# One Trainium2 core, a two-layer perceiver block: the first cross attention's queries widened from one stacked operand

## What is computed

```python
q_hk   = (layernorm(x) @ Wq.T).reshape(B, S, 16, 128)
q_big  = einsum('bshk,hkq->bshq', q_hk, w_kc_q)     # 384 wide
q_r    = einsum('bshq,hqr->bhsr', q_big, W_qr)      # 64 wide
k_r    = einsum('bld,hdr->bhlr', kv_r, W_kr)        # 64 wide
scores = einsum('bhsr,bhlr->bhsl', q_r, k_r)
```

## Time and profile before

| | |
|---|---|
| median of three runs | 2110.57 us |
| the profiled execution | 2113.88 us |
| its span, first to last instruction | 2112.1 us |
| mean granted TensorE clock | 0.982 of full speed |
| PE busy over the span | 94% |
| first queries (turning of rows to the last widen) | about 10 to 120 us |

### The profile page before, as it was taken

One profiled execution on the slowest core, in us unless ns is written; L12 is line 12 of the kernel. 1 busy time (PEld: TensorE's weight loads), 2 busy tenths in 40 slices (PEclk: granted clock), 3 DMA queues, 4 the chain that ended last, 5 costly groups with the idle time before them and its releaser, 6 DMA issues. The chain is left out here.

```text
span 2112.1 us, 29249 instructions
## 1 busy us (share of the span) xinstructions
PE 1982.2 (94%) x9274; PEld 1436.9 (68%) x9274; DVE 1202.1 (57%) x2691; ACT 868.3 (41%) x2163; POOL 1005.4 (48%) x928
## 2 busy tenths in 40 slices
PE   7989999999999999999997999989978999999996
PEld 6858998876688744666664899877755555555553
DVE  4577787467651022666656878769863343444444
ACT  3555555233312100344334555535514444454451
POOL 1257884212352100566667788475303444555552
PEclk9999999999999999999999999999988999999999
DMA  5552331200311100122134233210345999888886
GB/s 186 194 191 63 97 100 61 82 1 1 120 52 43 35 0 0 42 91 78 58 105 146 64 97 101 87 68 1 104 152 153 312 299 327 211 214 217 216 212 183
DMA packets 104948, 251.47 MB, mean 119 GB/s; under 512 B 14800, under 2 KB 40912, under 8 KB 96304
## 3 DMA queue, kind: packets, MB, share of 16 engines
q1 hardware_dynamic: 82224, 196.02, 27.5%
q0 software_dynamic: 21136, 51.11, 11.4%
q10 hardware_dynamic: 1440, 2.49, 0.3%
HBM read 279.44 MB, written 55.07 MB: 158 GB/s over the span
## 5 line engine op out<-in xcount | busy, mean ns | idle before, releaser
L99 PE MATMUL banks<-L1f_w,L1f_xT 128*128 x760 | 265.0, 492 | 1.8 <-issue 1.3
L2967 POOL DMA_INDIRECT moe_sums<-L1f_y,L1f_row x94 | 149.4, 1589 | 218.5 <-DVE L1f_is_who L2834 169.8
L99 PEld LDWEIGHTS banks<-L1f_w,L1f_xT 128*128 128x128 f32 x760 | 138.0, 192 | 81.6 <-issue 6.7
L160 POOL TENSOR_TENSOR rstd<-rstd,power 128x1 f32<-128x1 f32 x48 | 32.0, 667 | 221.4 <-DVE rstd L154 221.4
L2785 DVE SCALAR_TENSOR_TENSOR L1f_z<-banks,L1f_share,L1f_sg 128x192 f32<-128x192 f32 x95 | 39.7, 418 | 147.9 <-ACT L1f_sg L2718 146.9
L2975 POOL DMA_INDIRECT L1f_xg<-moe_rows,L1f_row x95 | 94.4, 993 | 61.5 <-DVE L1f_spare L2825 24.6
L2718 ACT ACTIVATE L1f_sg<-banks 128x192 f32<-128x192 f32 x95 | 31.4, 331 | 206.1 <-PE banks L99 143.3
L99 PE MATMUL banks<-L0f_down,L0f_z 128*128 128x512 f32 x256 | 111.1, 592 | 1.5 <-DVE L0f_z L2242 1.5
L99 PE MATMUL banks<-L0f_hT_hi,L0f_ug_hi 128*128 128x512 f32 x256 | 100.0, 391 | 0.0
L99 PE MATMUL banks<-L0f_hT_hi,L0f_ug_lo 128*128 128x512 f32 x256 | 99.6, 389 | 0.0
L99 PE MATMUL banks<-L0f_hT_lo,L0f_ug_hi 128*128 128x512 f32 x256 | 99.6, 389 | 0.0
(11 more groups left out here) (433 smaller groups left out, 5701.5 us busy)
## 6 DMA issues: line engine op xcount, KB each, us to landing
L1f_w<-in_experts SPq DMA_DIRECT2D x95, 1280.0 KB
L1f_laid<-moe_counts SPq DMA_DIRECT2D x59, 512.0 KB
w<-in_L1x_heads SPq DMA_DIRECT2D x16, 704.0 KB, 4.0
L0x_q<-L0x_far SPq DMA_DIRECT2D x20, 512.0 KB
L1x_q<-L1x_far SPq DMA_DIRECT2D x20, 512.0 KB
w<-in_L0x_heads SPq DMA_DIRECT2D x8, 1216.0 KB, 6.5
L0x_far<-L0x_away_far SPq DMA_DIRECT2D x8, 1024.0 KB
w<-in_wug SPq DMA_DIRECT2D x8, 1024.0 KB, 4.8
```

The costliest lines, as they stand in the source:

```text
L99: ins = pe.e.matmul(out, w, m, start=first and n == 0, stop=last and n == len(pairs) - 1)
L160: pool.e.tensor_tensor(self.rstd[:, i:i + 1], self.rstd[:, i:i + 1], self.power[:, 0:1], ALU.pow).then_inc(self.rstd_set.sem, 1)
L2967: pool.e.indirect_dma_start(self.sums[j % 2][:, :], bass.IndirectOffsetOnAxis(ap=self.row[:, j:j + 1], axis=0), self.y[j % self.NY][:], No ...
```

## The change

`qr_hi` and `qr_lo` of 128 rows are replaced by one operand per head of the pair, `qr[t][e]`: rows 0 to 63 hold the leading half of that head's q_r, rows 64 to 127 its remainder. So `qr_high` is two copies of 64 rows by 512 columns, and `qr_low` two subtractions of 64 rows by 512 columns (the second copy moves rows 64 to 127 to rows 0 to 63, the first subtraction the other way). The host packs `kr` twice, in rows 0 to 63 and 64 to 127. `widen` then takes two matmuls a head: `kr_hi` on all 128 rows by the stacked operand (hi by hi and hi by lo at once), and `kr_lo` on 64 rows by the stacked operand's upper 64 rows. `kr_lo` is made for 64 rows. Signals are counted twice as fast, to the same points. Order, banks, loads and sizes of loads are as before.

```diff
-            self.qr = [tuple(sb(f"qr_{v}{i}", [P, BANK], F32R) for v in ("hi", "lo")) for i in range(2)]
+            self.qr = [[sb(f"qr{i}_{e}", [P, BANK], F32R) for e in range(2)] for i in range(2)]
...
     def widen(self, pe, g, t):
...
-        pe.wait_ge(self.qr_hi, n + 1)
-        pe.wait_ge(self.qr_lo, n + 1)
+        pe.wait_ge(self.qr_hi, 2 * n + 2)
+        pe.wait_ge(self.qr_lo, 2 * n + 2)
...
+        hi, lo = self.kr[g % 2]
         for e in range(2):
-            ins = accumulate(pe, self.q_bank(t, e), parts(cut(self.kr[g % 2], slice(None), slice(e * DC, (e + 1) * DC)),
-                                                          cut(self.qr[t], slice(None))))
+            at, both = slice(e * DC, (e + 1) * DC), self.qr[t][e]
+            ins = accumulate(pe, self.q_bank(t, e), [(hi[:, at], both[:]), (lo[0:RR, at], both[0:RR, :])])
...
     def qr_high(self, act, g, t):
...
-        act.e.copy(self.qr[t][0][:], self.ask_bank(t)).then_inc(self.qr_hi.sem, 1)
+        for e in range(2):
+            act.e.copy(self.qr[t][e][0:RR, :], self.ask_bank(t)[e * RR:(e + 1) * RR, :]).then_inc(self.qr_hi.sem, 1)
...
     def qr_low(self, dve, g, t):
-        hi, lo = self.qr[t]
-        dve.wait_ge(self.qr_hi, 2 * g + t + 1)
-        dve.e.tensor_tensor(lo[:], self.ask_bank(t), hi[:], ALU.subtract).then_inc(self.qr_lo.sem, 1)
+        n = 2 * g + t
+        dve.wait_ge(self.qr_hi, 2 * n + 2)
+        for e in range(2):
+            both = self.qr[t][e]
+            dve.e.tensor_tensor(both[RR:P, :], self.ask_bank(t)[e * RR:(e + 1) * RR, :], both[0:RR, :],
+                                ALU.subtract).then_inc(self.qr_lo.sem, 1)
...
-            pool.e.tensor_tensor(lo[:], self.w(g, "kr").rearrange("p e n -> p (e n)"), hi[:], ALU.subtract).then_inc(self.kr_lo.sem, 1)
+            pool.e.tensor_tensor(lo[0:RR, :], self.w(g, "kr").rearrange("p e n -> p (e n)")[0:RR, :], hi[0:RR, :],
+                                 ALU.subtract).then_inc(self.kr_lo.sem, 1)
...
-            kr_t[1::2, RR:], kr_t[1::2, 0:RR] = kr_t[1::2, 0:RR].copy(), 0.0
+            kr_t[:, RR:] = kr_t[:, 0:RR]
```

More of the change, by code:

```diff
@@ L725, in __init__ @@
         self.asked, self.widened = take("asked", 2 * n), take("wide_again", 2 * n)
-        self.qr_hi, self.qr_lo = take("qr_hi", 2 * n), take("qr_lo", 2 * n)
+        self.qr_hi, self.qr_lo = take("qr_hi", 4 * n), take("qr_lo", 4 * n)
         self.query_signals()
@@ L792, in fold_ready @@
         if h == 0:
-            pe.wait_ge(self.qr_hi, 2 * n - 1)
-            pe.wait_ge(self.qr_lo, 2 * n - 1)
+            pe.wait_ge(self.qr_hi, 4 * n - 2)
+            pe.wait_ge(self.qr_lo, 4 * n - 2)
         elif h == 1:
@@ L873, in ask @@
         pe.wait_ge(self.h_lo, (t + 1) * NT // 2)
-        pe.wait_ge(self.qr_hi, 2 * (g - 1) + t + 1)
-        pe.wait_ge(self.qr_lo, 2 * (g - 1) + t + 1)
+        pe.wait_ge(self.qr_hi, 2 * (2 * (g - 1) + t + 1))
+        pe.wait_ge(self.qr_lo, 2 * (2 * (g - 1) + t + 1))
         accumulate(pe, self.ask_bank(t), [p for k in range(KD) for p in parts(
```

## The result

The changed kernel has a median of 2119.22 us (2115.99 to 2122.27, six runs) beside 2109.78 us of the kernel before in the same comparison: ratio 1.0046, 95% interval 1.0031 to 1.0062. Run again with the other experiments it had 2121.40 beside 2111.19, ratio 1.0051 (1.0034 to 1.0069). It is slower, by 9 to 10 us, where 5.6 were forecast. 2119.22 lies in the range, just under its upper end of 2120; the 2121.40 of the second comparison would lie above it. The time came into the range by a narrow margin.

A forecast was written before the change was run, and what follows sets the result against it. TensorE was taken to bound the stage from about 42 to 117 us. Pair 0 +0.8, widens up to ask(6, 0) +3.65, the write chain +0.97 and widen(7, 1) +0.15 gave +5.6 us: 2116.2 us, range 2108.5 to 2120.

The forecast's parts named there:

- Tile changes: In widen on TensorE, each switch between 128 and 64 rows costs 0.20 us; four make +0.35 us a widen net.
- A: Switches in widen cost nothing beside long matmuls: -4.05 us, 2106.5; chance 0.12.
- A2: Switches in widen cost half, 0.10 us each, so a widen stays level: +0.8 us in all, 2111.4; chance 0.10.
- B: Each switch in widen costs its upper price, 0.35 us: +0.96 a widen, +12.8 us, 2123.4; chance 0.10.
- a widen of 1.71 us: Timeline sign: widen takes 1.71 us to the next step's start, with starts about 0.33, 0.43, 0.43 and 0.43 apart.
- The 0.216 us: Skill page's distance between 512-column matmuls, by columns alone; by it 32 matmuls removed would gain 6.9 us.
- The 7.3 us saved: On TensorE, 16 widens drop from six matmuls to four: 32 fewer at 0.227 us each.
- Pair 0: At the stage's start, the longer split on ACT and DVE starts ask(0, 1) 0.9 us later; counted as +0.8 us.
- 64 rows cost what 128 do: ACT copies and DVE subtractions on 64 rows take as long as on 128, some 0.48 and 0.60 us back to back.
- Pair 7: At the stage's end, the chain through SP's write adds +0.97 us up to widen(7, 1), then +0.15 in it.
- the clock: TensorE is at 1.2 GHz from 31 to 34 us; if it recovers when it did, ask(0, 1)'s delay counts +0.8 us.
- The same: Outcome class of a time within about 0.3% (6.3 us) of the kernel before; chance 0.60, against slower 0.36, faster 0.04.

The follow-up runs named there:

- the grouped order: Changed kernel with widen's four products ordered 128, 128, 64, 64 rows, so two tile changes instead of four: 2116.58 us beside 2110.91, 1.0024.
- that order at pair 0: Changed kernel, second product on 128 rows; in pair 0 ACT and DVE split the last two row tiles before q_r of ask(0, 0): 2106.96 us beside 2110.82.
- the order at pair 7: 128-row second product and pair 0 reordered; in pair 7, q_r of ask(7, 1) split before keeping widen(6, 1)'s queries: 2105.19 us beside 2111.19.
- pair 0's order: Kernel before, only pair 0 reordered: ACT and DVE split the last two row tiles before q_r of ask(0, 0): ratio 0.9993.

## Why the forecast named the mechanism and came out too small

*Tile changes, 0.20 us each, four a widen:* right, in the middle pairs to the hundredth (12.05 us a pair), and shown by three kernels with the stacked operand that have zero, two and four of them (10.44, 11.27, 12.05 us), and by one that has them and nothing else of the change (12.95). Rivals A, A2 and B are out: they put a pair at 10.4, 11.3 and 13.3 us. One sign was written down wrong: a widen of 1.71 us "from its first start to the next step's" does not fit the four starts beside it, which add up to 1.62. Measured are 1.60, and the last 0.11 lies behind the fold's first start. (Rival B's +0.96 a widen should be +0.95; nothing hangs on it.) The 0.216 us that the prediction took from the Trainium skill's page "TensorE: Matmul & The Clock Gate", section "Back-to-back issue gap", is given there for an isolated matmul; for a stream of weight loads and matmuls the same section gives about 0.131 at 512 columns, which no run here shows. The stream measured 0.227.

*The 7.3 us saved are real:* without tile changes a pair is 0.91 us shorter. But only what is saved ahead of SP's write reaches the end. Behind it TensorE waits 4 us for the chain of write, copies and subtractions at pair 7.

*Pair 0, sized 0.9 us later:* the step that was too small is "64 rows cost what 128 do", with two operations back to back at "some 0.48 and 0.60 us". One operation costs that, but two on halves of the rows don't overlap with their neighbours. DVE from rows_lo(6) to rows_lo(7) is 31.09 - 28.93 = 2.16 us, where it was 1.21 before:

```profile
28.52 0.69 DVE L994 TENSOR_TENSOR L0x_hT_lo<-banks,L0x_hT_hi 128x512 fp32r<-128x512 f32 x1 [1.51 <-ACT L0x_hT_hi L928]
```

That is +0.95 instead of +0.6. On ACT the two copies take 1.19 us and the next starts when they have ended, 1.21 us after their start instead of 0.73: +0.48 where 0.3 were counted. Both figures are the same in the two profiles of the changed kernel. ask(0, 1) starts 1.4 us later than before in the first and 0.7 in the second, whose first asks came early.

*Pair 7, sized +0.97 up to widen(7, 1), measured +1.35* in both profiles: from widen(5, 1) to widen(7, 1) it is 126.14 - 108.11 = 18.03 us in the first, and 118.16 - 101.48 = 16.68 before:

```profile
101.48 0.39 PE L99 MATMUL banks<-L0x_qr_hi,L0x_kr_hi 128*128 128x512 f32 x1
```

The write takes the same 8.1 us (113.12 to 121.22). From its release to widen(7, 1) it is 4.92 us instead of 3.80: +1.12, where one more subtraction at 0.6 was counted. ACT's two copies come one after the other, DVE waits 0.28 us for them, and its two subtractions take 1.41.

*What had no term: the clock.* The sum let the clock in pair 0 come back as it had, and took for granted that it stays up elsewhere. In the first profile it fell to 1.2 GHz twice near the start, in pair 0's ask(0, 1) and again in ask(1, 0), behind gaps of 3.89 and 0.81 us, where the trace before has only the first. ask(1, 0), from its first matmul to the widen behind it, before and after:

```profile
41.91 0.47 PE L99 MATMUL banks<-L0x_hT_hi,L0x_mq_hi 128*128 128x512 f32 x1 [1.00 <-DVE L0x_mq_lo L1000]
...
44.71 0.39 PE L99 MATMUL banks<-L0x_qr_hi,L0x_kr_hi 128*128 128x512 f32 x1
```

```profile
43.44 0.68 PE L99 MATMUL banks<-L0x_hT_hi,L0x_mq_hi 128*128 128x512 f32 x1 [0.81 <-DVE L0x_mq_lo L1002]
...
47.85 0.39 PE L99 MATMUL banks<-L0x_qr,L0x_kr_hi 128*128 128x512 f32 x1
```

It takes 4.41 us instead of 2.80: 1.6 for the clock. In the second profile of the same kernel the clock stayed up there and fell at the end instead, right behind the wait at pair 7. One stretch of the first profile, then two of the second:

```profile
43.00:47.00 4.00, 3.56 (x9) 2.85 (x10) 0.29 (x1) 0.00 (x0) 0.01 (x1) 0.57 0.72 248
```

```profile
120.00:124.00 4.00, 2.74 (x10) 1.46 (x9) 3.62 (x5) 3.45 (x7) 0.00 (x0) 1.00 1.03 438
124.00:131.00 7.00, 7.00 (x10) 2.87 (x11) 4.96 (x8) 3.83 (x6) 4.85 (x7) 0.53 0.47 155
```

There the last widen and three fold_outs took 7.55 us (123.89 to the mark at 131.44), against 5.16 in the first profile (126.14 to 131.30): 2.4 us for the clock. At the mark +5.6 were forecast. With the sizes as measured it is +6.5 in the first profile and +5.9 in the second, and with 1.6 and 2.4 us of clock the 8.1 and 8.3 that the two marks show.

*The medians.* They stand 9.4 and 10.2 us above the kernel before, 1 to 2 us more than the mark shows, and the split alone costs 4.0 us in the median and 1.1 at its mark. One profile can't settle that. Behind the mark the code is the same in all thirteen profiles, and it takes from 1982.5 to 1991.1 us, with no order by kernel: the profile before has 1988.9 and the first one of the changed kernel 1982.5, so that their spans differ by 1.7 us only. The runs on record say more, since each has its mean granted clock. In the 84 runs of the kernel before that stand beside the experiments, the time goes with it (correlation -0.84), by about 1.7 us for each 0.001. The twelve runs of the changed kernel have 0.9805 in the mean, those 84 have 0.9820. By that slope some 2.7 us of their mean difference of 9.4 are clock, and 6.6 are left, near the corrected sum. The same estimate puts the split alone at +2.8 (2.4 expected), the second product on 128 rows at -3.6 (-3 expected, and no change in the medians), the grouped order at +0.7 (2 to 3 expected), and tile changes only at +11.1 (9 to 10 expected). It is an estimate from a correlation, good to a microsecond or two. Why the clock was lower in one kernel's runs than in another's is not shown.

So the time was in the range and most of the loss is the forecast mechanism. The distance from 5.6 to 9.4 is not: it is operations on half the rows, too cheap in the sum by 0.4 us at pair 7 and up to 0.6 at pair 0, and a clock for which there was no term. "The same" was the wrong likeliest class, because the sum stood 0.7 us under the 0.3% bound and what it left out added up in both profiles.

## What to carry to other kernels

Half of an operand is not half the work, and it can be more than the whole: on TensorE a 64-row product among 128-row ones costs 0.2 us at each change of tile, almost a matmul of 512 columns (0.227), and two changes if it stands alone. Fill the rows (here with the duplicate that was there anyway) or put products of one tile next to each other. A saving on the bounding engine counts only up to the next wait: look at what sits at the ends of the stage before counting it in full. Move the split that only the next pair needs behind the one that the engine waits for. With 128 rows and that order at pair 0 the change is faster than the kernel before, by 4 us, and with the order at pair 7 too by 6 (two comparisons, whose intervals overlap).

## What the runs showed of the hardware that was not expected

Two operations on DVE on different halves of the rows run one after the other. In pair 0 of the changed kernel rows_lo(6), the two 64-row subtractions and rows_lo(7) start 0.72 us apart each, which is 2.16 us in all, while 128-row ones follow at 0.60; with each half subtracted in place two take 1.40, nearly the same 1.41. The Trainium skill has it, on its page "VectorE: DVE Perf Modes", section "Two Vector instructions with no wait between them": an instruction whose input or output starts in another group of 32 rows than in the last instruction that read, or wrote, the same memory waits until all earlier ones have finished. The trace agrees, with those numbers. On ACT two 64-row copies take 1.18 to 1.19 us, where two 128-row ones take 1.07, and the next copy starts only when they have ended.

A wait of TensorE can cost more than its length. Ten of the thirteen profiles have a gap of 1.26 to 3.99 us ahead of widen(7, 1), and in nine of these the clock is at its lower level soon behind it (within 2 us), or already at its end; it cost up to 2.4 us. The other three, the kernel before (1.10), the same with pair 0's order (1.15) and the one with tile changes only (no gap), keep the full clock. But the length of the gap does not decide it. A gap of 1.26 us stands there in three profiles, and the clock fell in two of them. At the start of the stage it stayed up behind 2.11 us (tile changes only) and fell behind 0.81 us (the first profile of the changed kernel). What else decides it is not shown.
